# First four distances from PSUM, turns ahead of the values, nine product sums instead of six and another order of the taps

## What is computed

```python
v = (q @ W_value + b_value)
off = (q @ W_off + b_off)
attn = softmax(q @ W_attn + b_attn)           # over the 4 points
sampled = gather(x0, y0) * (1 - wx1) * (1 - wy1) + ...   # bilinear, 4 corners
out = (sampled * attn).sum(points) @ W_out + b_out + q
y = conv3x3(sign(out + move0), scale * sign(conv_w))
y = (y - mean) * gamma / sqrt(var + eps) + beta + out + move1
return where(y >= 0, y, a * y) + move2
```

## Time and profile before

| | us |
|---|---|
| median of 3 runs | 85.32 (85.08 to 85.67) |
| profiled execution, whole | 85.01 |
| its span | 83.2 |
| PE busy | 66.3 (80% of the span) |
| DVE busy | 58.9 (71%) |
| POOL busy | 47.7 (57%) |
| ACT busy | 46.2 (56%) |

### The profile page before, as it was taken

The page is one execution under the profiler, slowest core; times in us unless marked ns, Lnnn a source line. Parts: engine busy times, 40 slices in busy tenths (PEclk is TensorE's granted clock), DMA queues, the critical chain, the costliest instruction groups (busy, mean ns, idle before and its releaser), DMA issues.

```text
span 83.2 us, 1711 instructions
## 1 busy us (share of the span) xinstructions
PE 66.3 (80%) x642; PEld 25.9 (31%) x642; DVE 58.9 (71%) x85; ACT 46.2 (56%) x92; POOL 47.7 (57%) x47
## 2 busy tenths in 40 slices
PE   5999999899799999999999995999999984200000
PEld 4769257213243232232222321223233541200000
DVE  2304996999998999599796969738370087499910
ACT  1400799999199999999100089950000496159400
POOL 7980000579999999999999999991000000019000
PEclk9999999999999999999999999999999999985555
DMA  1918942960199991066001908285000000000294
GB/s 12 309 38 279 283 171 55 206 164 0 22 197 211 238 186 25 8 126 130 0 0 37 209 18 147 42 158 100 2 0 0 8 0 0 0 4 0 42 284 178
DMA packets 3897, 8.09 MB, mean 97 GB/s; under 512 B 560, under 2 KB 1584, under 8 KB 3888
## 3 DMA queue, kind: packets, MB, share of 16 engines
q1 hardware_dynamic: 2320, 4.40, 19.4%
q0 software_dynamic: 1120, 2.88, 19.2%
q10 hardware_dynamic: 448, 0.69, 2.8%
HBM read 2.27 MB, written 1.05 MB: 40 GB/s over the span
## 4 chain that ended last, share of the span: by engine, by line
PE 56%; DVE 18%; POOL 10%; issue 8%; ACT 2%; DVEq 1%; POOLq 0%
PE banks L530 21%; PE banks L513 12%; POOL ap L864 10%; DVE prod L970 4%; PE banks L562 4%; PE banks L580 4%; PE banks L466 3%; PE banks L476 3%; PE banks L508 3%; DVE prod L1104 3%; DVE prod L1115 2%; PE banks L459 2%; DVE bns L1075 2%; ACT sg L783 2%; DVE ays L941 1%
## 5 line engine op out<-in xcount | busy, mean ns | idle before, releaser
L864 POOL TENSOR_TENSOR ap<-ays,hat 128x512 f32<-128x512 f32 (+2 forms) x30 | 36.0, 1569 | 10.3 <-ACT hat L695 9.7
L970 DVE TENSOR_TENSOR prod<-banks,vpad 128x1024 f32<-128x1024 f32 (+2 forms) x20 | 22.1, 1111 | 6.9 <-PE banks L513 6.7
L530 PE MATMUL banks<-prod,wo 64*64 64x512 f32 (+2 forms) x208 | 23.0, 547 | 0.5 <-PE banks L530 0.5
L513 PE MATMUL banks<-ap,cst 32*64 32x512 f32 (+2 forms) x192 | 16.0, 568 | 1.0 <-POOL ap L864 1.0
L888 POOL TENSOR_SCALAR prod<-prod,prm,st 128x512 f32<-128x512 f32 x3 | 2.3, 765 | 18.3 <-ACT st L831 18.3
L970 DVE TENSOR_TENSOR prod<-banks,vswap 128x1024 f32<-128x1024 f32 (+3 forms) x13 | 12.6, 972 | 0.0
L530 PEld LDWEIGHTS banks<-prod,wo 64*64 64x64 f32 x208 | 6.9, 132 | 15.5 <-issue 11.0
L688 ACT ACTIVATE tab<-u,cst 128x512 f32<-128x512 f32 x12 | 8.3, 716 | 0.1
L513 PEld LDWEIGHTS banks<-ap,cst 32*64 32x64 f32 x192 | 4.1, 130 | 11.8 <-POOL ap L864 7.3
L871 POOL DMA_DIRECT2D prod<-prod x6 | 7.2, 1200 | 0.2 <-ACT hat L695 0.2
L695 ACT ACTIVATE hat<-tab 128x512 f32<-128x512 f32 x12 | 7.2, 622 | 0.0
(11 more groups left out here) (84 smaller groups left out, 82.7 us busy)
## 6 DMA issues: line engine op xcount, KB each, us to landing
prod<-prod POOLq DMA_DIRECT2D x4, 512.0 KB, 5.8
vswap<-vpad SPq DMA_DIRECT2D x4, 432.0 KB, 5.7
xs<-x_dram SPq DMA_DIRECT2D x3, 256.0 KB, 3.8
prod<-prod POOLq DMA_DIRECT2D x2, 384.0 KB, 5.6
out_dram<-prod SPq DMA_DIRECT2D x2, 256.0 KB, 3.2
wcf<-w_conv_dram SPq DMA_DIRECT2D x1, 288.0 KB, 4.1
wab<-w_abs_dram SPq DMA_DIRECT2D x1, 288.0 KB, 4.1
xs<-x_dram ACTq DMA_DIRECT2D x1, 256.0 KB, 2.8
```

The lines of the kernel that those rows point to most:

```text
L513: mm = pe.matmul(spread_into(t)[quadrant(i, g, t in SWAPPED)[1], g, 0:size_of(t)], sel_of(g)[rows_in, quadrant(i, g)[1]], weights_at(t)[ro ...
L530: mm = pe.matmul(into, wo[rows_in, rows_in], source, start=False, stop=last, skip_group_check=True)
L864: pool.tensor_tensor(into, factor, near, ALU.mult).then_inc(s_ap, 1)
L970: nc.vector.tensor_tensor(as_window(t, prod[:, t % PR, g, 0:n]), as_window(t, spread_into(t)[:, g, 0:n]), v_window(t, g), ALU.mult).then_i ...
```

## The change

On PE the turns of the upper half stand ahead of the upper values, and all logits of the lower half behind spread 0. ACT computes the distances for the first four hats from PSUM with the bias of the offsets (plus or minus one where the shift asks for it), then stores the values of one pair, and only then forms the upper positions. DVE computes only weight 0 and stores the values of the other pair; POOL computes weight 1 too. The upper values lie in other PSUM banks. There are 13 product buffers, a ring of one for DVE's weight, nine sums in place of six, and other tables of orders. Three taps more are added by transfers, so 23 units stand in place of 26.

```diff
-SUM_FROM = {1: 2, 5: 6, 8: 10, 16: 18, 20: 22, 24: 26}
-SUMS_BEHIND = {6: 1, 9: 5, 15: 8, 23: 16, 26: 20, 29: 24}
-DVE_COLUMNS = [2] + [0] * (ROWS - 1)
+SUM_FROM = {0: 1, 8: 2, 12: 10, 5: 4, 13: 9, 18: 16, 26: 24, 25: 17, 20: 22}
+SUMS_BEHIND = {7: 0, 11: 5, 13: 8, 18: 12, 19: 13, 24: 18, 26: 20, 28: 25, 30: 26}
+DVE_COLUMNS = [1] + [0] * (ROWS - 1)
+FROM_PSUM = [(0, 1, ZERO), (0, 0, ZERO), (0, 0, MINUS), (0, 0, PLUS)]
-        RA, RAP = 3, 6
+        RA, RAP = 1, 6
-        PR = 12
+        PR = 13
-        ps_v = [[bank[0], bank[1]], [bank[5], bank[4]]]
+        ps_v = [[bank[2], bank[3]], [bank[5], bank[4]]]
-        TAPS_AFTER = {7: [4], 9: [0, 3], 11: [9, 1], 13: [7], 15: [5, 12], 17: [15], 19: [14, 8], 21: [11], 23: [13],
-                      27: [16, 19, 23], 29: [17, 25, 27, 21], 31: [29]}
-        TAPS_AT_END = [24, 28, 30, 20, 31]
+        TAPS_AFTER = {9: [0, 6, 3], 11: [5, 7], 13: [11], 15: [8], 17: [14], 19: [15], 21: [12], 23: [13], 27: [21, 19, 23],
+                      29: [18, 20, 28], 31: [29, 25, 27]}
+        TAPS_AT_END = [30, 26, 31]
...
-            values(0)
             pe.wait_ge(s_sub, 2)
             logits_bias(2)
-            pe.wait_ge(s_x[1], 32)
-            logits(2, range(NCH // 2))
             pe.wait_ge(s_cst, 16)
             turn(0)
-            logits(2, range(NCH // 2, NCH))
-            pe.wait_ge(s_u, 2)
-            base_positions(1, 1)
+            values(0)
             for taps in SPREADS:
+                if taps[0] == 1:
+                    pe.wait_ge(s_x[1], 32)
+                    logits(2, range(NCH))
+                    pe.wait_ge(s_vp, G)
                 for t in taps:
                     spread(t)
                 if t == 1:
+                    pe.wait_ge(s_u, 2)
+                    base_positions(1, 1)
                     offsets(1, 1)
...
+                if (yh, d, k) in FROM_PSUM:
+                    act.wait_ge(s_off, POSITIONS.index((yh, d)) + 1)
+                    bias = prm[:, p_off + d:p_off + d + 1]
+                    if k != ZERO:
+                        act.wait_ge(s_bias, 2)
+                        bias = shifted_bias[:, k - MINUS:k - MINUS + 1]
+                    nc.scalar.activation(tab[:, n % 4], ps_off[yh][d][:], ACT.Abs, bias=bias).then_inc(s_abs, 1)
+                    return
...
-            act.wait_ge(s_prm, 16)
             positions(0, 1)
             positions(0, 0)
             act.wait_ge(s_cst, 16)
-            distances(0)
-            distances(1)
-            hats(0)
-            distances(2)
-            hats(1)
-            hats(2)
-            distances(3)
-            hats(3)
             hats(4)
...
-                pool.wait_ge(s_p, products_done(more, G - 1))
+                pool.wait_ge(s_p, products_done(max(into, more), G - 1))
...
-            store_upper_values()
             attend(0)
             weight(0)
-            weight(1)
-            softmax_max(2)
-            ROW_AFTER = [0, 3, 6, 7, 9, 9, 9]
+            store_upper_values()
+            ROW_AFTER = [0, 1, 4, 7, 8, 9, 9]
             for t in range(NT * YH):
                 product(t)
                 if t == 0:
+                    softmax_max(2)
+                if t == 1:
                     softmax_sub(2)
```

More of the change, by code:

```diff
@@ L166, in deformable_attention_then_binary_conv @@
         st = sb("st", [P, 17])
+        shifted_bias = sb("shifted_bias", [P, 2])
+        minus_one = sb("minus_one", [P, 1])
         spare = prod[:].rearrange("p r g n -> p (r g n)")
@@ L211, in deformable_attention_then_binary_conv @@
         s_abs = sem("abs_ready")
+        s_bias = sem("shifted_bias_ready")
         s_hat = sem("hats_ready")
@@ L719, in over, with store_values @@
                                      accum_out=over_sum[:, n:n + 1]).then_inc(s_ov, 1)
+            def store_values(g, yh, done):
+                nc.scalar.activation(values_of(g, yh), rows(ps_v[yh][g][:]), ACT.Identity,
+                                     bias=prm[:, p_bv:p_bv + 1]).then_inc(done, 1)
             def exponentials(part):
@@ L724, in exponentials @@
                 nc.scalar.activation(ex[:, yh, first:end], lsub[:, yh, first:end], ACT.Exp).then_inc(s_exp, 1)
+            act.wait_ge(s_prm, 16)
+            act.wait_ge(s_zero, 1)
+            act.wait_ge(s_top, 4)
+            for k in (MINUS, PLUS):
+                nc.scalar.activation(shifted_bias[:, k - MINUS:k - MINUS + 1], prm[:, p_off:p_off + 1], ACT.Identity,
+                                     bias=ones[:, 0:1] if k == MINUS else minus_one[:]).then_inc(s_bias, 1)
             exponentials(0)
             exponentials(1)
-            act.wait_ge(s_prm, 16)
+            distances(0)
+            distances(1)
+            hats(0)
+            hats(1)
+            distances(2)
+            hats(2)
+            act.wait_ge(s_zero, 2)
+            act.wait_ge(s_v, 1)
+            store_values(1, 0, s_vp)
+            distances(3)
+            hats(3)
             positions(0, 1)
@@ L751, in _ @@
             for g in range(G):
-                nc.scalar.activation(values_of(g, 1), rows(ps_v[1][g][:]), ACT.Identity,
-                                     bias=prm[:, p_bv:p_bv + 1]).then_inc(s_vlow, 1)
+                store_values(g, 1, s_vlow)
             for g in reversed(range(G)):
@@ L927, in store_upper_values @@
                 dve.wait_ge(s_v, 1)
-                for g in range(G):
-                    nc.vector.tensor_scalar(values_of(g, 0), rows(ps_v[0][g][:]), prm[:, p_bv:p_bv + 1], None,
-                                            ALU.add).then_inc(s_vp, 1)
+                nc.vector.tensor_scalar(values_of(0, 0), rows(ps_v[0][0][:]), prm[:, p_bv:p_bv + 1], None,
+                                        ALU.add).then_inc(s_vp, 1)
             def attend(n):
@@ L954, in product @@
                 yh, ky, kx = tap_of(t)
+                if t == 0:
+                    dve.wait_ge(s_vp, G)
                 if yh == 0 and ky == PLUS:
@@ L980, in _ @@
             nc.vector.memset(ones_b[:], 1.0).then_inc(s_top, 1)
+            nc.vector.memset(minus_one[:], -1.0).then_inc(s_top, 1)
             dve.wait_ge(s_prm, 16)
```

## The result

| | before | after |
|---|---|---|
| median | 85.25 (85.08 to 85.67, 4 runs) | 88.16 (87.84 to 88.55, 4 runs) |
| ratio of the times | | 1.036, 95% interval 1.031 to 1.041 |
| profiled execution, whole | 85.01 | 88.1 |
| its span | 83.2 | 86.3 |
| PE busy | 66.3 (80%) | 66.6 (77%) |

A forecast was written before the change was run, and what follows sets the result against it. POOL's weights and issues were taken to lead until PE's fixed tail; +0.6 on `prob` and +3.5 of issues put POOL's last weight 4.1 later, spread 30 2.5 later: profile 87.5, forecast 87.8 us, own range 86.9 to 88.7, with rivals 85.6 to 89.1.

The forecast's parts named there:

- (a): Kernel start up to POOL's `prob`: product 0 gains 1.4 us, not kept; `prob` starts at 22.85, 0.6 later.
- the sum: Total of the terms: +0.6 on `prob`, +3.5 issue time, 4.1 on POOL's last weight, +2.5 at spread 30.
- (b): POOL behind `prob`: nine issues cost 8.9 us where five cost 5.4; last weight at 60.5, before 56.38.
- (d): PE's waits for sums 0 and 5 to land: product 12 nearly 4 us late, but costing nothing while POOL is slower.
- (c): PE's end, following POOL's weights: spreads 30 and 31 start at 61.0, before 58.45, so the end moves 2.5 us.
- the cover: Slack at POOL's weight 18, which needs spread 12's buffer: 0.7 us before late landings would delay POOL.
- Rival 1: POOL's issues cost less, so POOL no longer leads: no change, +0.3, 85.6 us; chance 0.13.
- Rival 2: PE leads and three saved units come off the end: faster, 82.6 us; chance 0.12 with partial forms.
- partial forms: Weaker versions of rival 2's gain at PE's end, down to 84.4 us, counted within its chance of 0.12.
- Rival 3: Sum 5 lands 2 us later, breaking the cover; weight 18 and all behind slip 1.2 us: 89.1 us; chance 0.11.

The follow-up runs named there:

- the start alone: Kernel before given only the change's new start, keeping its six sums, order tables and twelve product buffers: 85.27 us, ratio 1.014.
- the short sums: Changed kernel with each of its nine accumulating transfers moving only 64 columns, issues and waits kept: 87.48 us, ratio 1.036.
- the kernel before with DVE weights: Kernel before, with DVE instead of POOL computing the first weight of the four lower rows: 93.17 us, ratio 1.097.
- the old start: Changed kernel's nine sums, order tables and 13 buffers on the start of the kernel before: 88.71 us, ratio of medians 1.040.

## Why the prediction was right

*(a) The start: right.* Product 0 at 14.75 (forecast 14.6), `prob` at 23.02 (22.85) after a wait of 2.09 us (2). That the gain is given back is borne out by the start alone: counted from DVE's `prob`, POOL's starts 12.2 us later with the new start and 11.5 with the old, 0.7 later where the sum had 0.6. With six sums this shows at the end: spread 30 is 0.7 later, and the ratios are 1.014 (0.999 to 1.028), 1.011 (1.004 to 1.018) and 1.012 (1.005 to 1.018), about 1 us.

*(b) The issues: right, and the term that carries the sum.* From `prob`'s end to the last weight 36.99 us, less 0.29 of waiting: 36.7 against 36.5. That the issues cost POOL their time at all is shown by the kernel without them, whose 25 weights took 27.79 and no more, and that it doesn't depend on the bytes by the short sums. The last weight came at 61.10 for 60.5: 0.1 from `prob`, 0.2 from the issues, 0.3 from the wait that (d) had put two weights later.

*(c) PE's end: right.* Weight 27 done at 54.63 for 54.0, spreads 30 and 31 at 61.62 for 61.0, 0.5 behind the last weight in both. The forecast's 2.5 us measured 3.2 by the profile, 2.9 by the medians.

*(d) The landings: the mechanism was right and its sizes were not.* I had the first landing at 31, product 12 at 38.9 and "covered", with 0.7 us in hand. The landing took 7.4 us, not about 6: the sentence that it may be read from the earlier trace rows took the highest row with `vswap` beside it (6.4) for the most that it can cost, and here sum 0 started in the same microsecond as the two transfers of the swapped values. Then came the clock, which no part of the sum had. Product 12 stood at 39.88. The second landing wait, put at 34.7 to 36.5, didn't come: with PE this late sum 5 was in. (A slip without weight: product 25, started at 51.8, would be done at 53.0 and not at 53.5, both ahead of 55.2.) So the cover was used up, and POOL waited 0.29 us. It cost 0.4 at spread 30 (48.3 against 47.9) because the two limits are nearly equal, which is luck of the sizes: the claim that late landings cost nothing "as long as POOL is the slow one" holds, but POOL was the slow one by less than a microsecond.

*Rival 1 (issues cost nothing) was mispriced.* It gave 85.6. With the issues really gone the time is 87.90. The landing and the clock stand behind, and the step that let it off at 85.6 was the same one of (d), "product 24 ends near 52.4": in that kernel product 24 started at 53.38 and ended at 54.6.

*Rival 2 was priced nearly right.* It named both its conditions, issues under 0.4 us and sum 0 about 3 us sooner, and 82.6 us. With both met (issues at zero, PE's first unit 28.2 after a first weight at 12.46, 4.2 sooner than in after, or 3.4 counted from the first weight), the time is 82.49. As a gain that is less than it had: 2.7 us off its 85.32, where the ratio of 0.978 makes 1.9. And it allowed for partial forms "down to 84.4", where one condition alone brings next to nothing: the runs give 87.5 and 87.9.

*Rival 3* asked for a landing of sum 5 2 us late. It was sum 0 that landed late, by 1.3 us (32.26 for 31), the clock added 1.0 to the units and 0.7 to spreads 10 and 11 (1.77 for 1.09), and all of it cost 0.4 at spread 30, a third of that rival's 1.3: product 12 came 1.0 late, hardly more than the cover.

## What to carry to other kernels

Price what an accumulating transfer takes on the engine that issues it (here 0.9 us, or 1.2 in two parts, however few bytes) before counting what it saves elsewhere, and place the issue in a wait of that engine: ahead of `prob`, where POOL waited, the same issue did not delay `prob`. When the trace shows a wait, take it away alone and together with the next candidate; two limits at one height each look harmless alone (0.4 and 0.6 us here) and hold 5.5 us between them.

## What the runs showed of the hardware

TensorE's granted clock fell to 0.50 behind waits of 2.90, 3.51 and 3.86 us in the middle of the kernel, and behind one of 3.95 us in the kernel before with DVE weights; it stayed at 1.00 behind one of 2.47 us. The 24 matmuls of three units took 3.33, 4.07 and 3.84 us against 2.38. So a wait for a transfer cost more than itself in three kernels, by up to 1.7 us.

One accumulating transfer of 512 KB between buffers in SBUF landed in 4.6 us alone and in 7.4 and 8.7 us when it started together with transfers of the swapped values (the 8.7 with the old start); the other eight sums of after landed in 4.7 to 6.1 us. Nine issues of 32 KB held POOL as long as nine of up to 512 KB (36.6 and 36.7 us from `prob` to the last weight, waits taken off).

A product of two SBUF tensors on VectorE took 0.69 us with POOL idle and up to 5.44 us beside POOL's weights, while one with an input from PSUM took 1.22 us beside them and 1.23 without.
